# Overrun tests in single steps, the flag read before the last store, the last two blocks finished one by one

## The chip, the cores and the metric

The kernel runs on one core of a Trainium2 chip. Its time is the device time of one execution in microseconds; of several runs the median counts. The core has TensorE (PE, matmuls; PEld is its weight load), VectorE (DVE), ScalarE (ACT) and GpSimd (POOL), and SyncE (SP), which issues DMAs here. Each engine works through a queue of its own in order, and they wait for each other by semaphores.

## The reference, cut to what matters

```python
h = jnp.maximum(_layernorm(x, axis=-1), 0.0)              # 6250 nodes x 128
agg = jax.ops.segment_sum(edge_attr, dst, num_segments=6250)   # 106250 edges x 128, dst sorted
y = jnp.concatenate([agg, h], axis=1)                     # 6250 x 256
hid = jax.nn.relu(y @ W1 + b1)                            # W1: 256 x 512
out = x + (hid @ W2 + b2)                                 # W2: 512 x 128
```

All of it is float32. Every node has 17 edges on average. Since `dst` is sorted, the edges of a node lie together, but the number of edges of a node depends on the data.

## The kernel before, in words

**The sums.** The edges are cut into 276 chunks of 384 and a rest of 266. Four chunks are a round (69 rounds and the rest, which makes 70). SP loads a round of 768 KB into one of 8 slots. For each chunk VectorE compares the edges' nodes, taken relative to the first node of the chunk, with 0 to 31 (a one-hot, line 481), and TensorE multiplies the one-hots with the edges (line 767). Each chunk yields sums for 32 nodes from its first node on. ScalarE copies them out of PSUM (line 390), TensorE turns them (line 778), and VectorE adds each chunk's 32 columns into `aggT` at a column that it has loaded into a register (line 570; the registers are loaded by `load_bases`, line 554).

**The steps.** Nodes are worked in 25 blocks of 256 (the last has 106). A loop over steps k = 1 to 24 runs on every engine, written out. In step k TensorE sums the rounds for block k, VectorE adds the sums of block k-1, splits its `aggT` into two parts, builds the one-hots for block k+1, takes the statistics of x for block k+2 and adds b2 to x of block k-1 (lines 633 to 650). The first three blocks are groups of their own, and from then on two blocks make a group, so there are NS = 14 groups. In the odd steps from 5 on TensorE runs layer 1 for a group: `layer1_h` (line 802), the turns of sums and of the next x, and `layer1_agg` (line 811). ScalarE applies ReLU to four parts of `hidden` (line 406). In the even steps TensorE runs layer 2 for that group (line 823) and VectorE adds x and writes `outrow` (`finish`, line 548), which SP stores. `outrow` is single for a pair of blocks, so `finish` waits for the store of the group before it.

**The order around the change.** If the data were such that a chunk spans more than 32 nodes, or the rounds taken for a block don't hold all its edges, the sums would be incomplete. Four tests find this out, on columns of `relA`, `relB`, `relC`, `relD` (`overrun`, line 587: a maximum, a minimum and three small operations, each waiting for the one before). VectorE does A in step 6, B in 7, C and D in 8, and a comparison of the bases (line 661) in 9. In step FLAG = 11 TensorE turns the resulting columns (lines 880 to 883), VectorE takes their maximum (line 667) and writes `flag`; TensorE waits for this maximum in the next step (line 855), as the PSUM bank is shared with layer 2's output. Every engine reads the flag into a register at its end and, if it is set, runs a slow second pass, which these inputs don't need. SP reads it after the last store has landed (lines 300 to 304).

**The end.** The last group holds block 23 and block 24 (53 rows of two nodes). After its layer 1, ScalarE writes four parts of hidden, layer 2 waits for all four (line 817) and writes both blocks into PSUM bank 5, VectorE adds them one after the other (line 543) and then signals once, and SP issues two stores (lines 266 and 267):

```python
sp.wait_ge(stored, 16 * (NS - ONES + 1))        # line 300
sp.wait_ge(flag_ready, 1)                       # line 302
again = sp.value_load(flag[0:1, 0:1], min_val=0, max_val=1)
with sp.If(again > 0):
```

Of the kernel before, what the change touches and what calls it, by code (L numbers as in the profile page):

```python
# [26 lines left out]
def graph_layer(nc, x, dst, edge_attr, W1, b1, W2, b2, out):  # L27
# [62 lines left out]
        return group1(k - 1)  # L90

    EARLY = ONES
    FLAG = 11
    assert group1(FLAG) is not None and group2(FLAG) is None

    def cols_of(s):
# [7 lines left out]
    with ExitStack() as ctx:  # L104
# [64 lines left out]
        hid_ps = [bank[3], bank[4], bank[6], bank[7]]  # L169
        out_ps = bank[5]  # L170
        row_ps = bank[5]
        misc_ps = bank[7]

        dst_landed = [sem(f"dst_landed{i}") for i in range(4)]
# [44 lines left out]
        hidden_ready = sem("hidden_ready")  # L219
        out_summed = sem("out_summed")  # L220
        out_added = sem("out_added")
        over_read = sem("over_read")
        stored_one = [sem(f"stored_one{i}") for i in range(2)]
        stored = sem("stored")
# [20 lines left out]
        @block.sync  # L245
        def _(sp):
            def load(r):
                if r >= RING:
                    sp.wait_ge(round_summed, r - RING + 1)
                slot = r % RING  # L250
                if r == NR:
                    sp.dma_start(edges[0:KREST, slot, 0:GR * F], rest_v).then_inc(edges_landed[slot], 16)
                else:
                    sp.dma_start(edges[:, slot, :].rearrange("p (t n) -> p t n", t=TILES),  # L254
                                 rounds_v[:, r, :, :]).then_inc(edges_landed[slot], 16)

            def load_x(b):
                if b - 3 >= 4:
                    sp.wait_ge(x_landed[b % 4], 16 * ((b - 3) // 4))
                sp.dma_start(xs[:, b, :], x_v[:, b, :]).then_inc(x_landed[b % 4], 16)  # L260

            def store(n, s):
                sp.wait_ge(out_added, n + 1)
                bs = blocks_of(s)
                if isinstance(s, int) and s == NS - 1:
                    sp.dma_start(out_v[:, bs[0], :], outrow[:, 0, :]).then_inc(stored, 16)
                    sp.dma_start(out_last_v, outrow[0:width(NB - 1), 1, :]).then_inc(stored, 16)
                elif len(bs) == 1:
                    sp.dma_start(out_v[:, s, :], outrow[:, s % 2, :]).then_inc(stored_one[s % 2] if n < NS else stored, 16)
                else:  # L270
                    sp.dma_start(out_v[:, bass.ds(bs[0], 2), :], outrow[:, :, :]).then_inc(stored, 16)

            sp.dma_start(dstA[:, :], dst[0:P * CHUNK].rearrange("(c e) -> c e", e=CHUNK)).then_inc(dst_landed[0], 16)
            load(0)
            load(1)
            sp.dma_start(w1[:, :, :], W1.rearrange("(t p) h -> p t h", p=P)).then_inc(w1_landed, 16)
            load(2)
            sp.dma_start(xs[:, 1:3, :], x_v[:, 1:3, :]).then_inc(x_next_landed, 16)
            load(3)
            load(4)  # L280
            sp.dma_start(w2[:, :, :], W2.rearrange("(t p) f -> p t f", p=P)).then_inc(w2_landed, 16)
            for r in range(5, RING):
                load(r)
            for k in range(NB):
                if 3 <= k + 3 < NB - 1:
                    load_x(k + 3)
                if k + 3 == NB - 1:
                    sp.dma_start(xs[0:NLAST // 2, NB - 1, :], x_last_v).then_inc(x_last_landed, 16)
                early = k <= EARLY + 1
                if early and group2(k - 1) is not None:  # L290
                    store(group2(k - 1), group2(k - 1))
                for r in ROUNDS[k]:
                    if r + RING < NROUNDS:
                        load(r + RING)
                if not early and group2(k - 1) is not None:
                    store(group2(k - 1), group2(k - 1))
            store(NS - 2, NS - 2)
            store(NS - 1, NS - 1)

            sp.wait_ge(stored, 16 * (NS - ONES + 1))  # L300

            sp.wait_ge(flag_ready, 1)
            again = sp.value_load(flag[0:1, 0:1], min_val=0, max_val=1)
            with sp.If(again > 0):
                with sp.Fori(0, FULL) as c:
                    sp.wait_ge(wide_summed, c * NWIDE + 1)
                    sp.dma_start(edges[:, 0:1, 0:G * F], chunks_v[:, bass.ds(c, 1), :]).then_inc(wide_landed, 16)
                sp.wait_ge(wide_summed, FULL * NWIDE + 1)
                sp.dma_start(edges[0:KREST, 0, 0:GR * F], rest_v).then_inc(wide_landed, 16)
                for s in range(ONES):  # L310
                    store(NS + s, s)
                with sp.Fori(ONES, NS - 1) as s:
                    store(NS + s, s)
                store(2 * NS - 1, NS - 1)
                sp.wait_ge(stored, 16 * (2 * NS - ONES + 2))
# [147 lines left out]
        def _(dve):  # L463
# [64 lines left out]
            def finish(n, s):  # L528
                bs = blocks_of(s)
                dve.wait_ge(out_summed, n + 1)  # L530
                if isinstance(n, int):
                    dve.wait_ge(residual_ready, min(bs[-1] + 1, NB))
                    if len(bs) == 1 and 2 <= n < ONES:
                        dve.wait_ge(stored_one[n % 2], 16 * (n // 2))
                    if n == ONES:
                        dve.wait_ge(stored_one[0], 16 * ((ONES + 1) // 2))
                        dve.wait_ge(stored_one[1], 16 * (ONES // 2))
                    if ONES < n < NS:
                        dve.wait_ge(stored, 16 * (n - ONES))
                if isinstance(s, int) and s == NS - 1:  # L540
                    for i, b in enumerate(bs):
                        w = width(b)
                        ins = nc.vector.tensor_tensor(outrow[0:w, i, :], out_ps[0:w, i * 2 * F:(i + 1) * 2 * F],
                                                      xs[0:w, b, :], ALU.add)
                elif len(bs) == 1:
                    ins = nc.vector.tensor_tensor(outrow[:, s % 2, :], out_ps[:, 0:2 * F], xs[:, s, :], ALU.add)
                else:
                    ins = nc.vector.tensor_tensor(outrow[:, :, :], out_ps[:, :].rearrange("p (b f) -> p b f", b=2),
                                                  xs[:, bass.ds(bs[0], 2), :], ALU.add)
                ins.then_inc(out_added, 1)  # L550
# [33 lines left out]
                                      misc_ps[:, 0:G * CC].rearrange("p (g c) -> p g c", c=CC)).then_inc(done, 1)  # L584
                nc.vector.tensor_copy(relT_rest[0:KREST, :], misc_ps[0:KREST, 64:64 + GR]).then_inc(done, 1)

            def overrun(col, rel, lim):
                link(nc.vector.tensor_reduce(col[:, 1:2], rel[:, :], AX_X, ALU.max))
                link(nc.vector.tensor_reduce(col[:, 2:3], rel[:, :], AX_X, ALU.min))
                if lim is None:  # L590
                    link(nc.vector.tensor_scalar(col[:, 3:4], col[:, 0:1], float(-MEAN), float(FULL * CHUNK - SLACK),
                                                 ALU.mult, ALU.add))
                else:
                    link(nc.vector.scalar_tensor_tensor(col[:, 3:4], col[:, 0:1], float(-MEAN), lim, ALU.mult, ALU.add))
# [38 lines left out]
            for k in range(1, NB):  # L633
# [15 lines left out]
                    stats(k + 2)  # L649
                add_b2(k - 1)  # L650
                if k == 6:
                    dve.wait_ge(limit_ready, 1)
                    overrun(colA, relA, limit[:, 0:1])
                if k == 7:
                    overrun(colB, relB, limit[:, 1:2])
                if k == 8:
                    overrun(colC, relC, limit[0:CC, 2:3])
                    overrun(colD, relD, None)
                if k == 9:
                    apart = w1[0:1, 0, 0:FULL - 1]  # L660
                    link(nc.vector.tensor_tensor(apart, base_tab[:, 2:FULL + 1], base_tab[:, 0:FULL - 1],
                                                 ALU.subtract))
# [67 lines left out]
        def _(pe):  # L730
# [83 lines left out]
            def layer2(n, s):  # L814
                if not (isinstance(n, int) and n == 0):
                    pe.wait_ge(out_added, n)
                pe.wait_ge(hidden_ready, n * HT + HT)
                at = 0
                for i, b in enumerate(blocks_of(s)):
                    w = width(b)  # L820
                    for j in range(2):
                        for t in range(HT):
                            ins = nc.tensor.matmul(out_ps[0:w, (2 * i + j) * F:(2 * i + j + 1) * F],  # L823
                                                   hidden[:, t, at:at + w], w2[:, t, :], start=(t == 0), stop=(t == HT - 1))
                        at += w
                ins.then_inc(out_summed, 1)

            pe.wait_ge(ident_ready, 1)
            pe.wait_ge(rel_ready, 1)
# [116 lines left out]
```

## Time and profile before

| | us |
|---|---|
| median of 3 timed runs | 218.17 |
| lowest, highest | 218.01, 219.18 |
| the profiled execution's own time | 217.2 |
| its span | 215.2 |
| TensorE busy | 193.9 |
| VectorE busy | 132.2 |
| ScalarE busy | 84.6 |
| GpSimd busy | 43.1 |

The page gives busy times as shares of the span. The span leaves out some 2 us that the execution's own time has. TensorE's matmuls in float32 show as two records for one instruction, so a group of layer 2 with 16 products has 32 records. The granted clock of TensorE is 0.991 of full speed over the span, which is the higher of its two levels (2.4 GHz) nearly throughout.

### The profile page before, as it was taken

How to read it: one execution, taken by the hardware profiler on the slowest of the kernel's cores; microseconds unless marked ns; L12 is line 12 of the kernel's file. 1: busy time of each engine (PE TensorE's matmuls, PEld its weight loads, DVE VectorE, ACT ScalarE, POOL GpSimd, SP SyncE). 2: the span in 40 equal slices, each digit the busy share in tenths (PEclk: the TensorE clock that was granted, in tenths of full speed). 3: DMA queues.
4: the chain of work that ended last, by engine and by line, in shares of the span. 5: the costliest groups of instructions: out<-in, count | busy, mean ns of one | idle time of the engine just before them, and what ended most of it. 6: DMA issues, size and time to landing. Idle time of an engine off the chain costs nothing.

```text
span 215.2 us, 6776 instructions
## 1 busy us (share of the span) xinstructions
PE 193.9 (90%) x2549; PEld 164.8 (77%) x2549; DVE 132.2 (61%) x581; ACT 84.6 (39%) x185; POOL 43.1 (20%) x120
## 2 busy tenths in 40 slices
PE   1396999889999999699999999999999999999970
PEld 1264878778788797498798898887988988978860
DVE  1945664648767977977488577477574774741210
ACT  3031445071663532443713713734436138333400
POOL 5554020221122202102202222022022211200000
PEclk9999999999999999999999999999999999999996
DMA  6899999999999999999989999989999960100101
GB/s 222 280 389 362 375 376 374 377 379 382 388 374 387 376 381 384 376 329 309 343 266 381 345 347 377 323 296 387 293 379 373 312 225 16 49 3 0 49 5 39
DMA packets 44623, 62.55 MB, mean 291 GB/s; under 512 B 1795, under 2 KB 44294, under 8 KB 44588
## 3 DMA queue, kind: packets, MB, share of 16 engines
q1 hardware_dynamic: 44116, 61.66, 82.0%
q10 hardware_dynamic: 472, 0.43, 0.8%
q8 instruction: 22, 0.36, 0.7%
q14 instruction: 13, 0.11, 0.1%
HBM read 58.88 MB, written 3.20 MB: 288 GB/s over the span
## 4 chain that ended last, share of the span: by engine, by line
PE 64%; DMA 12%; DVE 11%; SPq 4%; issue 3%; ACT 3%; DVEq 2%; ACTq 0%
PE bank L823 17%; PE bank L767 16%; PE bank L802 13%; PE bank L811 13%; DMA edges<-in_edge_attr 7%; DMA xs<-in_x 5%; SPq L254 3%; PE bank L778 2%; DVE aggT L570 2%; DVE onehot L481 2%; PE bank L788 2%; DVEq L554 1%; ACT agg_hi L396 1%; DVE agg_lo L523 1%; ACT hidden L406 1%
## 5 line engine op out<-in xcount | busy, mean ns | idle before, releaser
L767 PE MATMUL bank<-edges,onehot 128*32 128x128 f32 x1656 | 55.1, 285 | 5.1 <-DMA edges<-in_edge_attr 4.3
L767 PEld LDWEIGHTS bank<-edges,onehot 128*32 128x32 f32 x1656 | 45.4, 114 | 12.9 <-issue 6.1
L823 PE MATMUL bank<-w,hidden 128*128 128x128 f32 (+1 forms) x400 | 48.3, 278 | 1.3 <-ACT hidden L406 0.7
L823 PEld LDWEIGHTS bank<-w,hidden 128*128 128x128 f32 (+1 forms) x400 | 45.6, 189 | 4.2 <-issue 3.2
L406 ACT ACTIVATE hidden<-bank,b_col 128x512 f32<-128x512 f32 (+2 forms) x56 | 34.2, 635 | 35.9 <-PE bank L811 35.8
L570 DVE TENSOR_TENSOR aggT<-bank,aggT 128x32 f32 x277 | 35.2, 189 | 14.3 <-issue 6.9
L375 ACT ACTIVATE xn<-xs,shift,rstd 128x128 f32<-128x128 f32 (+1 forms) x50 | 21.7, 485 | 44.1 <-POOL shift L331 44.1
L324 POOL TENSOR_SCALAR var<-meanvar 128x2 f32<-128x2 f32 (+1 forms) x25 | 7.4, 294 | 135.2 <-DVE meanvar L501 135.2
L481 DVE TENSOR_TENSOR onehot<-relT,iota 128x384 f32<-128x384 f32 x69 | 34.4, 551 | 0.0
L802 PE MATMUL bank<-hT_hi,w_hi 128*128 128x512 f32 (+2 forms) x56 | 22.4, 399 | 0.0
L517 DVE TENSOR_TENSOR hT_lo<-bank,hT_hi 128x256 fp32r<-128x256 f32 (+1 forms) x25 | 10.4, 415 | 19.3 <-ACT hT_hi L382 19.3
L811 PE MATMUL bank<-agg_hi,w_hi 128*128 128x512 f32 (+2 forms) x56 | 21.4, 382 | 0.1
L802 PE MATMUL bank<-hT_lo,w_hi 128*128 128x512 f32 (+2 forms) x56 | 20.8, 371 | 0.0
L802 PE MATMUL bank<-hT_hi,w_lo 128*128 128x512 f32 (+2 forms) x56 | 20.7, 370 | 0.0
L811 PE MATMUL bank<-agg_hi,w_lo 128*128 128x512 f32 (+2 forms) x56 | 20.4, 364 | 0.0
L811 PE MATMUL bank<-agg_lo,w_hi 128*128 128x512 f32 (+2 forms) x56 | 20.3, 363 | 0.0
L396 ACT ACTIVATE agg_hi<-aggT 128x256 fp32r<-128x256 f32 (+1 forms) x25 | 10.7, 429 | 20.3 <-DVE aggT L570 20.3
L329 POOL TENSOR_TENSOR rstd<-var,power 128x2 f32<-128x2 f32 (+1 forms) x25 | 17.7, 709 | 2.1
L523 DVE TENSOR_TENSOR agg_lo<-aggT,agg_hi 128x256 fp32r<-128x256 f32 (+1 forms) x25 | 10.5, 419 | 9.4 <-ACT agg_hi L396 9.4
L496 DVE BATCH_NORM_STATS2 halves<-xs 128x6 f32<-128x128 f32 (+1 forms) x50 | 11.9, 280 | 5.7 <-DMA xs<-in_x 5.7
L778 PE MATMUL bank<-ident,sums 128*128 128x128 f32 x70 | 12.4, 284 | 3.1 <-DVE aggT L570 1.6
L390 ACT ACTIVATE sums<-bank 128x384 f32<-128x384 f32 (+3 forms) x25 | 11.7, 466 | 6.9 <-PE bank L767 5.8
(93 smaller groups left out, 169.0 us busy)
## 6 DMA issues: line engine op xcount, KB each, us to landing
edges<-in_edge_attr SPq DMA_DIRECT2D x69, 768.0 KB, 8.9
xs<-in_x SPq DMA_DIRECT2D x21, 128.0 KB, 8.9
out_rows<-outrow SPq DMA_DIRECT2D x10, 256.0 KB
w<-in_L_gnn_W SPq DMA_DIRECT2D x1, 512.0 KB, 9.7
out_rows<-outrow SPq DMA_DIRECT2D x4, 128.0 KB, 8.4
xs<-in_x SPq DMA_DIRECT2D x1, 256.0 KB, 11.4
w<-in_L_gnn_W SPq DMA_DIRECT2D x1, 256.0 KB, 12.8
hidden<-in_dst SPq DMA_DIRECT2D x1, 192.0 KB, 3.2
```

Of the source, the lines that this page charges most:

```text
L329: nc.gpsimd.tensor_tensor(rstd[0:w, par, :], var[0:w, par, :], power[0:w, :], ALU.pow).then_inc(pow_ready, 1)
L375: ins = nc.scalar.activation(xn[0:w, par, j, :], xs[0:w, b, j * F:(j + 1) * F], ACT.Relu, bias=shift[0:w, par, j:j + 1], scale=rstd[0:w, p ...
L396: nc.scalar.activation(agg_hi[:, halves].rearrange("f (j p) -> f j p", j=2), aggT[:, bass.ds(b * BLOCK, halves.stop - halves.start)].rearr ...
L406: nc.scalar.activation(hidden[:, t, 0:cols], hid_ps[t][:, 0:cols], ACT.Relu, bias=b1_col[:, t:t + 1]).then_inc(hidden_ready, 1)
L481: nc.vector.tensor_tensor(hot, of.unsqueeze(2).to_broadcast([p, n, W]), iota[0:p, 0:W].unsqueeze(1).to_broadcast([p, n, W]), ALU.is_equal) ...
L523: nc.vector.tensor_tensor(split(agg_lo[:, halves]), aggT[:, bass.ds(b * BLOCK, halves.stop - halves.start)].rearrange("f (p j) -> f j p", ...
L570: nc.vector.tensor_tensor(win, turn_ps[:, at:at + W], win, ALU.add).then_inc(agg_added, 1)
L767: ins = nc.tensor.matmul(sums_ps[t * W:(t + 1) * W, cols], onehot[:, hots, e, :], edges[:, slot, e * F:(e + 1) * F], start=(g == 0), stop= ...
L778: ins = nc.tensor.transpose(turn_ps[:, i * F:i * F + rows], sums[0:rows, k % 2, i * F:(i + 1) * F], ident[0:rows, 0:rows])
L802: nc.tensor.matmul(hid_ps[t][:, 0:cols], wt[:, 1, to], v[:, here], start=(i == 0), stop=False)
L811: ins = nc.tensor.matmul(hid_ps[t][:, 0:cols], wt[:, 0, to], v[:, 0:cols], start=False, stop=(i == 2))
L823: ins = nc.tensor.matmul(out_ps[0:w, (2 * i + j) * F:(2 * i + j + 1) * F], hidden[:, t, at:at + w], w2[:, t, :], start=(t == 0), stop=(t = ...
```

## The change

`FLAG` goes from 11 to 19. The four tests are cut into their maximum (`overrun_top`), their minimum (`overrun_low`) and the three small operations (`overrun_limit`), which do the same as before, and stand in steps 6 to 16; the comparison of the bases goes to step 17. SP reads the flag before the last group's stores. In the last group the second block goes to PSUM bank 1 (`last_ps`, else used for the turned sums), with semaphores of its own, so that each block is added and stored by itself. In every layer 2 the first four products each wait for their own part of `hidden`.

```diff
-    FLAG = 11
+    FLAG = 19
...
+        last_ps = turn_ps
...
                     sp.dma_start(out_v[:, bs[0], :], outrow[:, 0, :]).then_inc(stored, 16)
+                    sp.wait_ge(last_added, 1 if n < NS else 2)
                     sp.dma_start(out_last_v, outrow[0:width(NB - 1), 1, :]).then_inc(stored, 16)
...
             store(NS - 2, NS - 2)
-            store(NS - 1, NS - 1)
-
-            sp.wait_ge(stored, 16 * (NS - ONES + 1))
-
             sp.wait_ge(flag_ready, 1)
             again = sp.value_load(flag[0:1, 0:1], min_val=0, max_val=1)
+            store(NS - 1, NS - 1)
+
+            sp.wait_ge(stored, 16 * (NS - ONES + 1))
             with sp.If(again > 0):
...
                 if isinstance(s, int) and s == NS - 1:
-                    for i, b in enumerate(bs):
-                        w = width(b)
-                        ins = nc.vector.tensor_tensor(outrow[0:w, i, :], out_ps[0:w, i * 2 * F:(i + 1) * 2 * F],
-                                                      xs[0:w, b, :], ALU.add)
-                elif len(bs) == 1:
+                    w = width(bs[1])
+                    nc.vector.tensor_tensor(outrow[:, 0, :], out_ps[:, 0:2 * F], xs[:, bs[0], :],
+                                            ALU.add).then_inc(out_added, 1)
+                    dve.wait_ge(last_summed, 1 if n < NS else 2)
+                    nc.vector.tensor_tensor(outrow[0:w, 1, :], last_ps[0:w, 0:2 * F], xs[0:w, bs[1], :],
+                                            ALU.add).then_inc(last_added, 1)
+                    return
+                if len(bs) == 1:
...
                 if k == 6:
+                    overrun_top(colA, relA)
+                if k == 7:
+                    overrun_low(colA, relA)
+                if k == 8:
                     dve.wait_ge(limit_ready, 1)
-                    overrun(colA, relA, limit[:, 0:1])
-                if k == 7:
-                    overrun(colB, relB, limit[:, 1:2])
-                if k == 8:
-                    overrun(colC, relC, limit[0:CC, 2:3])
-                    overrun(colD, relD, None)
+                    overrun_limit(colA, limit[:, 0:1])
                 if k == 9:
+                    overrun_top(colB, relB)
+                if k == 10:
+                    overrun_low(colB, relB)
+                if k == 11:
+                    overrun_limit(colB, limit[:, 1:2])
+                if k == 12:
+                    overrun_top(colC, relC)
+                if k == 13:
+                    overrun_low(colC, relC)
+                if k == 14:
+                    overrun_limit(colC, limit[0:CC, 2:3])
+                if k == 15:
+                    overrun_top(colD, relD)
+                    overrun_low(colD, relD)
+                if k == 16:
+                    overrun_limit(colD, None)
+                if k == 17:
                     apart = w1[0:1, 0, 0:FULL - 1]
...
             def layer2(n, s):
                 if not (isinstance(n, int) and n == 0):
                     pe.wait_ge(out_added, n)
-                pe.wait_ge(hidden_ready, n * HT + HT)
+                ends = isinstance(s, int) and s == NS - 1
                 at = 0
                 for i, b in enumerate(blocks_of(s)):
                     w = width(b)
+                    o = last_ps if ends and i else out_ps[:, 2 * i * F:2 * (i + 1) * F]
...
                     for j in range(2):
                         for t in range(HT):
-                            ins = nc.tensor.matmul(out_ps[0:w, (2 * i + j) * F:(2 * i + j + 1) * F],
-                                                   hidden[:, t, at:at + w], w2[:, t, :], start=(t == 0), stop=(t == HT - 1))
+                            if i == 0 and j == 0:
+                                pe.wait_ge(hidden_ready, n * HT + t + 1)
+                            ins = nc.tensor.matmul(o[0:w, j * F:(j + 1) * F], hidden[:, t, at:at + w], w2[:, t, :],
+                                                   start=(t == 0), stop=(t == HT - 1))
                         at += w
-                ins.then_inc(out_summed, 1)
+                    if ends and i == 0:
+                        ins.then_inc(out_summed, 1)
+                ins.then_inc(last_summed if ends else out_summed, 1)
```

## Rows read from the trace of the kernel before

**Rows 1.** The page: busy us (share) of TensorE; layer 2's weight loads, mean ns.

```profile
PE 193.9 (90%) x2549; PEld 164.8 (77%) x2549; DVE 132.2 (61%) x581; ACT 84.6 (39%) x185; POOL 43.1 (20%) x120
...
L823 PEld LDWEIGHTS bank<-w,hidden 128*128 128x128 f32 (+1 forms) x400 | 45.6, 189 | 4.2 <-issue 3.2
```

**Rows 2.** Windows: us, busy us of each engine, granted clock, DMA share, GB/s.

```profile
170.00:200.00 30.00, 30.00 (x348) 25.72 (x347) 16.46 (x78) 11.78 (x26) 4.27 (x12) 1.00 0.23 80
```

**Rows 3.** Who waited for whom, TensorE, 20 to 200 us: total, times, longest.

```profile
PE bank L778 <- DVE aggT L570: 1.6, 1, 1.6
...
PE bank L767 <- DVE over L667: 0.5, 1, 0.5
```

**Rows 4.** Windows again: the same work of TensorE in step 9 and step 11.

```profile
83.06:91.54 8.48, 6.75 (x34) 4.87 (x30) 6.96 (x31) 3.91 (x8) 1.12 (x4) 1.00 1.06 375
99.36:105.67 6.31, 6.31 (x32) 5.03 (x31) 3.60 (x14) 3.69 (x8) 1.43 (x4) 1.00 0.99 350
```

**Rows 5.** The chain of waits, steps 6 to 8: start us, us, what.

```profile
65.70 0.47 DVE colA L588
66.20 0.56 DVE colA L589
...
73.85 0.47 DVE colB L588
...
75.50 0.87 DVEq L554
...
81.66 0.46 DVE colC L588
...
84.57 0.71 DVEq L554
```

**Rows 6.** Timeline of VectorE: start us, us, operation [idle before <- releaser].

```profile
68.27 0.69 DVE L548 TENSOR_TENSOR outrow<-bank,xs 128x512 f32<-128x512 f32 x1 [0.92 <-DMA out_rows<-outrow]
...
76.58 1.69 DVE L570 TENSOR_TENSOR aggT<-bank,aggT 128x32 f32 x12 [1.08 <-issue]
...
92.61 1.69 DVE L570 TENSOR_TENSOR aggT<-bank,aggT 128x32 f32 x12 [1.10 <-issue]
...
107.82 1.69 DVE L570 TENSOR_TENSOR aggT<-bank,aggT 128x32 f32 x12 [0.93 <-issue]
```

**Rows 7.** The chain of waits, the end.

```profile
202.51 2.07 ACT hidden L406 x4
...
204.72 3.92 PE bank L823 x32
208.66 0.33 DVE outrow L543
209.00 0.41 DVE outrow L543
```

**Rows 8.** Timeline of SP, the last stores.

```profile
209.43 0.35 SPq L266 DMA_DIRECT2D out_rows<-outrow  x1
209.83 0.29 SPq L267 DMA_DIRECT2D out_rows<-outrow  x1
```

**Rows 9.** Lines 303, 304: count, ns min/median/max, first and last start us.

```profile
L303 SPq TENSOR_LOAD <-flag x1: 465/465/465, 214.0 to 214.0; - x1
...
L304 SPq COMPARE_BRANCH  x1: 45/45/45, 214.8 to 214.8; - x1
```

**Rows 10.** Windows while only the last store runs.

```profile
212.00:213.00 1.00, 0.00 (x0) 0.00 (x0) 0.00 (x0) 0.00 (x0) 0.00 (x0) 0.50 0.07 22
```

**Rows 11.** Line 757, TensorE's queue: the waits for one-hots.

```profile
L757 PEldq EVENT_SEMAPHORE  x70: 51/51/51, 6.5 to 190.3; - x70
```

**Rows 12.** The chain of waits, around the start of a layer 2.

```profile
91.61 1.45 PE bank L767 x48
93.05 3.77 PE bank L823 x32
```

**Rows 13.** Line 890: TensorE's branch on the flag.

```profile
L890 PEldq COMPARE_BRANCH  x1: 3529/3529/3529, 207.6 to 207.6; - x1
```

More of the change, by code:

```diff
@@ L221, in graph_layer @@
         out_added = sem("out_added")
+        last_summed = sem("last_summed")
+        last_added = sem("last_added")
         over_read = sem("over_read")
@@ L297, in _ @@
             store(NS - 2, NS - 2)
+            sp.wait_ge(flag_ready, 1)
+            again = sp.value_load(flag[0:1, 0:1], min_val=0, max_val=1)
             store(NS - 1, NS - 1)
             sp.wait_ge(stored, 16 * (NS - ONES + 1))
-            sp.wait_ge(flag_ready, 1)
-            again = sp.value_load(flag[0:1, 0:1], min_val=0, max_val=1)
             with sp.If(again > 0):
@@ L585, in turned_cd, with overrun_top, overrun_low, overrun_limit @@
                 nc.vector.tensor_copy(relT_rest[0:KREST, :], misc_ps[0:KREST, 64:64 + GR]).then_inc(done, 1)
-            def overrun(col, rel, lim):
+            def overrun_top(col, rel):
                 link(nc.vector.tensor_reduce(col[:, 1:2], rel[:, :], AX_X, ALU.max))
+            def overrun_low(col, rel):
                 link(nc.vector.tensor_reduce(col[:, 2:3], rel[:, :], AX_X, ALU.min))
+            def overrun_limit(col, lim):
                 if lim is None:
@@ L820, in layer2 @@
                     w = width(b)
+                    o = last_ps if ends and i else out_ps[:, 2 * i * F:2 * (i + 1) * F]
+                    if ends and i and n >= NS:
+                        pe.wait_ge(last_added, 1)
                     for j in range(2):
                         for t in range(HT):
-                            ins = nc.tensor.matmul(out_ps[0:w, (2 * i + j) * F:(2 * i + j + 1) * F],
-                                                   hidden[:, t, at:at + w], w2[:, t, :], start=(t == 0), stop=(t == HT - 1))
+                            if i == 0 and j == 0:
+                                pe.wait_ge(hidden_ready, n * HT + t + 1)
+                            ins = nc.tensor.matmul(o[0:w, j * F:(j + 1) * F], hidden[:, t, at:at + w], w2[:, t, :],
+                                                   start=(t == 0), stop=(t == HT - 1))
                         at += w
-                ins.then_inc(out_summed, 1)
+                    if ends and i == 0:
+                        ins.then_inc(out_summed, 1)
+                ins.then_inc(last_summed if ends else out_summed, 1)
             pe.wait_ge(ident_ready, 1)
```

## The prediction

> **What bounds the kernel now.** The busy table first: TensorE is busy 90% of the span [rows 1]. The windows then show a stretch from 170 to 200 us in which it is busy 30.00 of 30.00 us at a granted clock of 1.00 [rows 2]. The list of waits for TensorE between 20 and 200 us gives one large pause, 1.6 us at line 778 (the turn of a block's sums) for a VectorE add at line 570, and one of 0.5 us for the flag's reduction at line 667 [rows 3]. From the 1.6 us pause to the end TensorE has almost no gap, and the list's one row for the edges' DMA (0.4 us, once) lies at 20.6 us, before the pauses. So a microsecond that TensorE loses before about 92 us is a microsecond of the end, and so is whatever follows its last matmul. I look for the change's effect in three places: that pause, the tail after 202 us, and the cost of the new waits.
>
> **The pause in step 9.** The same work (four groups of layer 1 for x, the turns, four groups for the sums) fills 83.06 to 91.54, 8.48 us, in step 9 and 99.36 to 105.67, 6.31 us, in step 11 [rows 4]. TensorE is busy only 6.75 of the 8.48 us. The difference, 8.48 - 6.31 = 2.17 us, is the 1.6 us pause and the refilling after it. Why is VectorE late there? The chain of waits goes through it [rows 5]: in step 6 the test on colA from 65.70; in step 7 the test on colB from 73.85 to 75.50, where loading the bases starts, 1.65 us, and colA's five operations are the same; in step 8 colC and colD from 81.66 to 84.57, 2.91 us. All of it stands in front of the output add and the add of the sums that TensorE waits for.
>
> The change leaves colA's maximum, 0.47 us, in step 6, its minimum, 0.56 us, in step 7, and in step 8 the three small operations on colA, about 0.6 us with their gaps. The saving is 1.18 us in step 6, 1.09 in step 7, 2.3 in step 8. The first doesn't survive: the output add at 68.27 waited 0.92 us for the store that frees its buffer [rows 6], and would start at the same time. The others add up: VectorE is 1.1 + 2.3 = 3.4 us earlier at the end of step 8's tests. The sums of step 8 then are added by about 87.6 - 3.4 = 84.2 us, where TensorE wants them at 86.1 (its turn began at 87.76, after a pause of 1.63). Margin 1.9 us: the whole 2.17 us goes, and what is late next in step 9 is TensorE itself. Bounds: 0 if something else holds VectorE there (below), 2.2 if all goes; no reason lets it cost. I take 2.17.
>
> What the pieces cost where they land: 0.5 to 0.6 us in each step from 9 to 14, two reductions in 15 (0.35 + 0.45 us), about 0.5 in 16, about 1.1 in 17. VectorE runs two steps without tests in about 16.0 - 2.9 - 1.1 = 12.0 us (its adds of sums started at 76.58 and 92.61 [rows 6], and the tests of step 8 and 9 stood between), TensorE takes some 14.1 to 14.8 us for two. 12.0 + 1.2 stays below it, so the cover is some 1 us for each pair of steps and they cost nothing. Without that cover they would cost what they take, 7.3 us of tests in all less the 1.6 us left in steps 6 to 8: 5.7 us. Nothing in the windows points to that end.
>
> The flag's reduction moves from step 11 to 19 with its 0.5 us wait [rows 3] and its three transposes. VectorE waits in step 11 until TensorE has turned the columns and adds the sums only at 107.82 [rows 6], while TensorE asks for the next turn at 112.46: 3 us spare. Step 19 has the same rounds and blocks, so it repeats this. Cost 0; bounds -0.5 to +0.5 us.
>
> SP's queue: the loads keep their order, the only thing moved past them is the flag, and SP reaches it after its store at 200 us, when flag_ready is long set.
>
> **The tail.** ScalarE writes the four parts of hidden from 202.51 on in 2.07 us, 0.52 us each; TensorE starts layer 2 at 204.72, 0.14 us after the last [rows 7]. Its own layer 1 ends near 203.9. The 32 records from 204.72 are 16 products of two records each, 3.92 / 16 = 0.245 us for one. With waits part by part, the first is free to start once layer 1 leaves the array (about 203.9; part 0 is there at 203.1), the second follows at 204.1, the third at 204.3 (part 2 at 204.1 plus 0.14), and the fourth at 204.72 as before. Three products leave the path: 0.70 us. Less is possible if a restart costs; 0 to 0.74 (the pause), I take 0.70.
>
> Behind the last matmul the old order is: add of the first block at 208.66, 0.33 us, add of the second 0.41 us [rows 7], first store issued at 209.43, second at 209.83 [rows 8]. New: the first block's sums are complete after 8 products, near 206.1 us, its add and its store (0.35 us) run while TensorE does the second block, and bank 1 holds the second, so the two don't meet. After the last matmul stand only the second add, 0.41 us, and the second store. That removes 0.33 + 0.40 = 0.73 us. Of the first block's add the wait is new, and nothing stands behind it on VectorE but the second add; behind SP's new wait stands only the last store. Bounds 0.4 (if the first store were to run late) to 0.73; I take 0.73, since its slot is 2 us early.
>
> The flag. After the last store has landed SP loads the flag at 214.0 for 0.465 us, and branches at 214.8 [rows 9]: 0.80 us, on the path by themselves, and now done between 200.8 and 206 us. Bounds 0.4 to 0.8; I take 0.80.
>
> The last store itself: issued at 209.83, landed at 213.99, 4.16 us. While it runs the DMA engines' share is 0.07 at 22 GB/s [rows 10], that is one engine of 16. 53 KB at 22 GB/s are 2.5 us, and what is left of 3.4 us between the end of the first store's burst and 213.8 is about 0.9 us of other traffic on that engine. The shape is unchanged, so I keep 4.16, with 0.9 us to either side.
>
> In the Trainium skill (DMA: Bandwidth & Descriptors, "Why a DMA increments its semaphore by 16 and not by 1") the number of engines is the largest one up to 16 that divides the row count, so 53 rows get one; the trace agrees. [...]
>
> **The new waits.** Layer 2 runs 14 times, and 13 times its four parts are long ready, so 3 x 13 = 39 waits are added that are met. A wait of line 757 is a 51 ns instruction on TensorE's queue, 70 of them [rows 11]. Bounds: 0 and 39 x 0.051 = 2.0 us. I take 0: two rounds of sums took 1.45 us with waits between them, and layer 2 followed at 93.05, where 91.61 + 1.45 = 93.06 ends the round before, in spite of two waits between [rows 12].
>
> **Sum.** 2.17 + 0.70 + 0.73 + 0.80 = 4.40 us. The profiled execution took 217.2 us (its span is 215.2), so it would be 212.8. It lies 1 us below the median of the timed runs, 218.17; taking the sum from that gives 213.8 us.
>
> **Rivals.**
> A, the pause stays: VectorE in step 8 is held by something other than the tests. For: the output add in step 8 waits for a store too, and that of step 6 did [rows 6]. Against: that store was issued at 71 us, 11 us before. Only the tail is gained: 218.17 - 2.23 = 215.9. Chance 0.12.
> B, the last store lands late: its one engine meets other traffic, since TensorE's branch (3.529 us, [rows 13]) fetches code in the same microseconds. The price is the 0.9 us above, and the result 214.7. Chance 0.13.
> C, the branch of SP: TensorE's takes 3.529 us [rows 13] where SP's took 0.045 [rows 9]. With the flag read early, SP might pay it after its last wait: 213.8 + 3.5 = 217.3. Against: SP idles about 4 us ahead of it in both kernels. Chance 0.05. The Trainium skill (Runtime: NRT & Kernel Launch, "Instruction fetch mechanics") says that a taken branch to a page not yet held forces a fetch by DMA; TensorE's row agrees, SP's shows none.
> D, slower: each wait between the parts keeps the next weight load from going ahead, in all 13 other layer 2s. The price is one load of 0.189 us [rows 1] for each of 39 waits, 7.4 us, and the time 213.8 + 7.4 = 221.2; it decides the sign from 4.4 / 39 = 0.11 us a wait. Against: no gap at 93.05. Chance 0.04. The rule behind it: the Trainium skill (TensorE: Matmul & The Clock Gate, "Architectural detail: the array is 16× 32×32, not 1× 128×128") says that TensorE's queue can pull a weight load ahead of matmuls in flight. Whether a met wait stops that, no page says; the rounds of line 767 speak against it.
>
> **How the numbers follow.** The forecast has 0.66. About 0.5% (1.1 us) is what a measurement can tell from no change. Faster by more than that: the forecast, A and B, 0.91; within: C, 0.05; slower: D, 0.04. The range goes down to 212.7 (the store's 0.9 us, and 0.2 for the spread of the runs) and up to 216.2 (A with 0.3), leaving out C, D and B together with A.
>
> **What would show it.** Step 9 from its layer 1 to its last sum is 6.3 us, with no wait of line 778 for an add. In the tail six records of layer 2 stand before the fourth ScalarE part has ended, with a gap behind them; the last add is a single one of 0.41 us; the last store is issued some 0.02 us after it ends, where it used to be 0.42; nothing but a branch follows its landing. The length of layer 2 in mid-kernel (3.77 us [rows 12]) shows D: unchanged if I am right, over 4 us if not. I am wrong if TensorE waits for VectorE in steps 9 to 20 by more than 0.5 us in all, or if the landing takes over 5 us.

## The result, and the profile after

The changed kernel took 212.59 us (median of 4 runs, 212.05 to 212.94) beside 218.09 us for the kernel before (4 runs, 217.35 to 219.18). The ratio is 0.9742 with a 95% interval of 0.9695 to 0.9788: faster by 2.6%. The forecast was 213.8 us in a range from 212.7 to 216.2. The direction was right; the time came out 0.1 us below the range.

The profiled execution took 212.71 us with a span of 210.5 us, where the one before took 217.2 and 215.2. That is 4.5 us less, and the forecast's sum was 4.40. So most of the miss is not in the change's terms but in the number that they were taken from, as the experiments show.

The windows of the changed kernel over steps 9 and 11, the same work as in [rows 4]:

```profile
82.92:89.22 6.30, 6.30 (x33) 4.93 (x37) 4.79 (x26) 3.01 (x6) 1.42 (x4) 1.00 1.06 376
96.97:103.28 6.31, 6.31 (x34) 4.93 (x37) 4.65 (x23) 3.01 (x6) 1.39 (x4) 1.00 1.05 373
```

Step 9 now takes what step 11 takes, 6.30 us in place of 8.48. Its list of waits for TensorE between 20 and 200 us has no row in which line 804 (the turn of the sums, 778 before) waits for a VectorE add; the flag's wait is there as in [rows 3]:

```profile
PE bank L804 <- ACT sums L393: 0.7, 3, 0.2
PE bank L793 <- DVE over L693: 0.5, 1, 0.5
```

The timeline of VectorE, lines 554 (output add), 576 (adds of the sums) and the first pieces of the tests, answers to [rows 6]:

```profile
65.41 0.55 DVE L594 TENSOR_REDUCE colA<-relA 128x1 f32<-128x384 f32 x1
67.84 0.69 DVE L554 TENSOR_TENSOR outrow<-bank,xs 128x512 f32<-128x512 f32 x1 [1.89 <-DMA out_rows<-outrow]
...
73.34 0.55 DVE L597 TENSOR_REDUCE colA<-relA 128x1 f32<-128x384 f32 x1
...
82.13 0.69 DVE L554 TENSOR_TENSOR outrow<-bank,xs 128x512 f32<-128x512 f32 x1 [1.26 <-DMA out_rows<-outrow]
82.74 1.58 DVE L576 TENSOR_TENSOR aggT<-bank,aggT 128x32 f32 x12
```

In step 6 the time saved goes into the wait for the store, 1.89 us where it was 0.92. In step 8 the output add waits for a store as well, 1.26 us, for a store issued at 70.97 us. Yet the sums are added by 84.3 us, 1.6 us before TensorE asks for them at 85.92.

The end of the chain of waits, then SP's timeline, then SP's and TensorE's branches (lines 307 and 923), for [rows 7 to 9] and [rows 13]:

```profile
199.62 1.99 PE bank L837 x12
201.62 3.93 PE bank L854 x32
...
205.57 0.42 DVE outrow L548
```

```profile
204.14 0.35 SPq L269 DMA_DIRECT2D out_rows<-outrow  x1
206.02 0.28 SPq L271 DMA_DIRECT2D out_rows<-outrow  x1
```

```profile
L307 SPq COMPARE_BRANCH  x1: 45/45/45, 210.1 to 210.1; - x1
...
L923 PEldq COMPARE_BRANCH  x1: 3689/3689/3689, 204.5 to 204.5; - x1
```

Layer 2 follows layer 1 with no gap, one add of 0.42 us stands behind it, the last store is issued as it ends, and the branch follows the landing at 210.1. From the last matmul's end to the last store it was 1.2 us, now 0.47.

### The profile page after: what moved, and what is told of

The parts are those of the page before. It is cut to its first block, busy times and chain, and to the rows that moved or that the text cites. A ratio compares the mean times of both kernels' runs of the same rounds, so it can differ in the third digit from the quotient of the medians.

```text
span 210.5 us, 6775 instructions
## 1 busy us (share of the span) xinstructions
PE 193.7 (92%) x2549; PEld 164.9 (78%) x2549; DVE 131.5 (62%) x581; ACT 84.7 (40%) x185; POOL 43.0 (20%) x120
## 4 chain that ended last, share of the span: by engine, by line
PE 79%; DMA 11%; SPq 3%; DVE 2%; ACT 1%; issue 1%; DVEq 0%; ACTq 0%
PE bank L854 21%; PE bank L793 20%; PE bank L828 16%; PE bank L837 15%; DMA edges<-in_edge_attr 6%; DMA xs<-in_x 5%; PE bank L804 3%; SPq L257 3%; PE bank L814 2%; PE bank L786 1%; ACT xn L378 1%; DVE aggT L576 1%; SPq L282 0%; ACT sums L393 0%; SPq L280 0%
## 5 line engine op out<-in xcount | busy, mean ns | idle before, releaser
L828 PEld LDWEIGHTS bank<-hT_hi,w_hi 128*128 128x128 f32 x56 | 10.9, 194 | 4.2 <-issue 2.8
```

The lines of the kernel that those rows point to most:

```text
L828: nc.tensor.matmul(hid_ps[t][:, 0:cols], wt[:, 1, to], v[:, here], start=(i == 0), stop=False)
```

## The experiments

Times are medians with the range of the runs. Each group of kernels ran on one chip, with runs of the kernel before beside it; ratios are against those. The first group (e0, e1, e6, e2) had 20 runs of the kernel before, median 217.17 us. The second (a0, e3, e4, e8) had 11 with 218.0, the third (x1, x2, x3, d1) 11 with 217.17, the fourth (v1, e8 again) 17 with 218.45.

**e0, the kernel before against itself.** No edit.

> The kernel before once more, against itself. Theory 1 (the terms of the profile, 4.7 us in all, are the gain, and the 5.5 us between the medians carry 0.8 us of scatter of the kernel before): its median comes out nearer to the profiled 217.2 us than to 218.1, and the pause at the turn of the sums in step 9 is 1.6 us again. Theory 2 (the pause differs from execution to execution, and the profiled one had a short one): a pause clearly other than 1.6 us, and spans of the timed runs that scatter by over 1 us.

Measured: 217.31 us (216.64 to 219.13, 12 runs), ratio 1.0018 (0.9986 to 1.005), pause 1.7 us in the profile. Both theories got something: the median is 0.8 us below that of the first comparison, and the runs spread over 2.5 us in two heaps. Of all 71 timed runs of the kernel before in these experiments, 45 took 216.3 to 218.1 us (median 216.93), and 26 took 218.3 to 219.6 (median 218.78). In time alone the gap between the heaps is only 0.2 us wide; the clock parts them better. The upper 26 all have a mean granted clock of 0.982 to 0.989, of the lower 45 all but two have more than 0.989.

**e1, the tests back in steps 6 to 9.**

```diff
 # on the changed kernel
-                if k == 6:
-                    overrun_top(colA, relA)
-                if k == 7:
-                    overrun_low(colA, relA)
...
+                if k == 6:
+                    dve.wait_ge(limit_ready, 1)
+                    overrun(colA, relA, limit[:, 0:1])
+                if k == 7:
+                    overrun(colB, relB, limit[:, 1:2])
+                if k == 8:
+                    overrun(colC, relC, limit[0:CC, 2:3])
+                    overrun(colD, relD, None)
+                if k == 9:
```

> The changed kernel with the tests of A to D back in steps 6 to 8 and the bases' comparison in 9 (the flag's step stays 19). Theory 1: the pause of step 9 is back and the time rises by 2.2 us over the changed kernel, to about 214.8 us, some 2.5 to 3 us below the kernel before. Theory 2: by over 3 us. Rival 3 (the pause had another cause than the tests): no change, 212.6.

Measured: 215.28 us (214.74 to 218.02, 9 runs), ratio 0.9914 (0.9877 to 0.9952). The runs are again in two heaps, five from 214.7 to 215.3 us and three from 216.5 to 217.4, and two of these three have a clock of 0.987 or less. The ninth, 218.02 us at 0.979, is left out of the ratio. The lower heap is 2.2 us above the changed kernel (212.69, median of its 10 runs in both groups), the upper 4 us. Rival 3 is out.

The ninth run is the profiled one, and its trace shows what the pause can do. First TensorE's longest wait, then windows (the granted clock is the third column from the right), then the chain of waits:

```profile
PE bank L784 <- DVE aggT L576: 1.9, 1, 1.9
```

```profile
88.00:91.00 3.00, 2.38 (x10) 1.84 (x11) 2.71 (x13) 1.02 (x2) 0.00 (x0) 0.85 1.06 373
91.00:95.00 4.00, 4.00 (x48) 3.08 (x50) 2.70 (x16) 2.48 (x6) 1.47 (x4) 0.69 0.69 248
95.00:100.00 5.00, 5.00 (x68) 4.63 (x64) 3.75 (x12) 1.32 (x5) 0.82 (x3) 1.00 0.80 247
```

```profile
89.36 4.61 PE bank L817 x12
```

TensorE waits 1.9 us for the sums and starts again at 88.5. The clock then stands at 0.50 (1.2 GHz) from about 90.1 to 93.5 us, and the twelve products of layer 1 take 4.61 us where they take 2.75 in the changed kernel: 1.86 us more. That is the distance between the heaps of before, 218.78 - 216.93 = 1.85 us. As an estimate, 3.4 us at half the clock lower the mean over 215 us by 0.008, beside median clocks of 0.994 and 0.988 in the two heaps.

**e6, only the tests spread, on the kernel before.**

```diff
 # on the kernel before
-    FLAG = 11
+    FLAG = 19
 # and the tests as in the change, steps 6 to 17
```

> The kernel before with only the tests spread over steps 6 to 17 and the flag in step 19. Theory 1: 2.2 to 2.4 us less than before, some 215.8 us beside 218.1. Theory 2: over 3 us less. Rival 3: nothing.

Measured: 214.94 us (214.45 to 215.35, 6 runs), ratio 0.9879 (0.9849 to 0.991), which is 2.6 us with an interval of 2.0 to 3.3. By the medians of the group it is 2.2 us, against the lower heap of before 2.0. This edit moves the flag's step as well; e1, which leaves it at 19, gives 2.2 us for the tests alone. One heap is left, 0.9 us wide. No run of any kernel here without the pause had a mean clock under 0.990, in 64 runs of nine kernels.

**d1, a longer pause.**

```diff
 # on the kernel before
                 if k == 8:
+                    for _ in range(8):
+                        link(nc.vector.tensor_reduce(colC[:, 1:2], relC[:, :], AX_X, ALU.max))
                     overrun(colC, relC, limit[0:CC, 2:3])
```

> The kernel before with eight more reductions in step 8, 0.56 us each, so that the pause of TensorE in step 9 is 1.6 + 4.5 = 6.1 us. Theory 2 (a pause also costs clock behind it): the granted clock falls to its lower level after the pause, the products behind it take up to twice as long, and the time rises by 4.5 us and 1.5 to 2 us more, to 223 us or more. Theory 1 (a pause costs its length alone): 217.0 + 4.5 = 221.5 us.

Measured: 223.28 us (222.16 to 223.92, 6 runs), ratio 1.0271 (1.0233 to 1.0309), every run at a clock of 0.975 to 0.981. Windows of its profile; the granted clock is the third column from the right:

```profile
86.00:89.00 3.00, 0.03 (x1) 0.00 (x0) 2.72 (x10) 0.00 (x0) 0.00 (x0) 1.00 1.06 378
89.00:92.00 3.00, 0.00 (x0) 0.00 (x0) 1.98 (x13) 0.00 (x0) 0.00 (x0) 0.64 1.05 371
92.00:94.00 2.00, 1.63 (x7) 1.56 (x8) 1.82 (x6) 0.44 (x1) 0.00 (x0) 0.50 0.79 286
94.00:96.00 2.00, 2.00 (x6) 1.54 (x5) 1.83 (x9) 0.69 (x1) 0.91 (x3) 0.50 0.11 38
96.00:98.00 2.00, 2.00 (x15) 1.38 (x17) 0.90 (x7) 1.47 (x3) 0.56 (x2) 0.84 0.01 2
```

and its chain of waits there:

```profile
92.37 0.87 PE bank L780 x3
93.24 0.43 PE bank L790 x2
93.67 4.20 PE bank L813 x12
```

TensorE is idle from 86 to 92.4 us, the clock falls to 0.50 (1.2 GHz) within the pause and stays there until after 96. The three turns take 0.87 us where they take 0.33, the twelve products 4.20 where they take 2.75. That is 0.5 + 0.2 + 1.45 = 2.2 us behind the pause. Against the lower heap of before the time rose by 6.35 us, for 4.5 us of reductions and a pause 4.7 us longer: some 1.7 to 1.9 us is the clock's. Theory 2 holds. The Trainium skill (TensorE: Matmul & The Clock Gate, "What's actually happening") says that a monitor of the array's activity halves its clock after idleness; the trace agrees, 0.50 within a pause of 6.3 us.

That the upper heap of the kernel before is this fall behind its own pause has good support. e1's trace shows the fall behind the same pause, at the price of 1.86 us; the heap has that size and the lower clock, and it goes with the pause. What is not shown is the fall in the kernel before itself: its four profiles (the first, e0, b1 and b2) have pauses of 1.6, 1.7, 1.8 and 1.5 us, and are all of the lower heap at a clock of 1.00 in step 9. What decides between a fall and none is open.

A rival for the heap is a fall near the start. e1's trace has one at 22 to 25 us too, behind waits of 0.7 and 1.0 us. The trace of e8 run again (below) has one at 24.5 to 28, behind a wait of 2.3 us, and v1's has one at 24 to 28, behind a wait of 2.5. These need no pause in step 9. But in the 64 runs without that pause they are rare enough that none has a clock under 0.990, where 28 of the 71 runs of the kernel before have one, so they don't make the heap.

**b1 and b2, two more profiles of the kernel before.** No edit.

> A look at one execution of the kernel before. If it is one above 218.3 us (three in ten were), theory 2 expects a granted clock under 1.00 in the 6 us behind the pause of step 9 and 1.5 to 2 us more for the products there; theory 1 expects the time elsewhere. If it is below, it tells nothing new.

> One more execution of the kernel before, for the same: above 218.3 us, theory 2 expects the clock to fall behind the pause of step 9, and theory 1 the time elsewhere; below, it tells nothing new.

Measured: 217.09 and 216.57 us, both of the lower heap, with pauses of 1.8 and 1.5 us and no fall of the clock behind them.

**e2, the flag read late again.**

```diff
 # on the changed kernel
-            sp.wait_ge(flag_ready, 1)
-            again = sp.value_load(flag[0:1, 0:1], min_val=0, max_val=1)
             store(NS - 1, NS - 1)

             sp.wait_ge(stored, 16 * (NS - ONES + 1))
+            sp.wait_ge(flag_ready, 1)
+            again = sp.value_load(flag[0:1, 0:1], min_val=0, max_val=1)
```

> The changed kernel with SP's load of the flag after the last store's landing again. Theory 1: 0.75 to 0.8 us more than the changed kernel, about 213.4 us. A rival: under 0.3 us, if the load can hide behind something else at the end.

Measured: 212.82 us (212.78 to 213.6, 6 runs), ratio 0.9796 (0.9765 to 0.9827), span 210.9. The lowest span is 0.9 us above the changed kernel's 210.0, the time only 0.1 above its 212.69. A surprise: what the span leaves out is 1.8 to 1.9 us here and 1.9 to 2.8 us in the changed kernel.

**e3, one wait for all four parts.**

```diff
 # on the changed kernel
+                pe.wait_ge(hidden_ready, n * HT + HT)
                 ends = isinstance(s, int) and s == NS - 1
...
-                            if i == 0 and j == 0:
-                                pe.wait_ge(hidden_ready, n * HT + t + 1)
```

> The changed kernel with layer 2 waiting for all four parts of hidden at once, as before. The prediction's term: 0.70 us more than the changed kernel (its trace shows 0.73), 12.9 to 13.0 beside 212.2. Rival: the wait by parts costs in the other 13 layer 2s and this kernel gets back part of it, so less than 0.5 us.

(The figures "12.9 to 13.0" there stand for 212.9 to 213.0.) Measured: 213.20 us (212.78 to 213.45), ratio 0.9775 (0.9724 to 0.9827). That is 0.5 us above the changed kernel's 212.69, but level with the 213.17 that it had in the same group (a0, below), so the time alone doesn't show the term. The median span does, 211.05 beside 210.5. Its chain of waits ends

```profile
199.97 2.07 ACT hidden L409 x4
202.04 0.14 issue
202.18 3.92 PE bank L853 x32
```

The gap before layer 2 is back, and in mid-kernel a layer 2 takes 3.77 us in both: the 39 waits that are met cost nothing.

**e4, the last two blocks together.**

```diff
 # on the changed kernel: PSUM, adds, signal and stores of the last group as in the kernel before
-                    o = last_ps if ends and i else out_ps[:, 2 * i * F:2 * (i + 1) * F]
+                    o = out_ps[:, 2 * i * F:2 * (i + 1) * F]
```

> The changed kernel with the last two blocks in one PSUM bank, added one after the other, signalled once and then stored. The prediction's term: 0.73 us more than the changed kernel, and the last store is issued 1.17 us after the last matmul's end where the changed kernel has 0.47. Rival: the last store's landing is what counts, and it gets shorter when it follows another store at once, so less than 0.4 us.

Measured: 213.29 us (212.65 to 213.82), ratio 0.9778 (0.9725 to 0.983): 0.6 us above 212.69 and 0.1 above 213.17, with a median span of 211.25 us. In its profile the last store goes out 1.19 us after the last matmul, against 0.47:

```profile
206.64 0.35 SPq L269 DMA_DIRECT2D out_rows<-outrow  x1
207.04 0.33 SPq L270 DMA_DIRECT2D out_rows<-outrow  x1
```

**e8, the last store cut into 48 and 5 rows.**

```diff
 # on the changed kernel (the new semaphore is waited for with the other)
-                    sp.dma_start(out_last_v, outrow[0:width(NB - 1), 1, :]).then_inc(stored, 16)
+                    w = width(NB - 1)
+                    cut = w - w % 16
+                    sp.dma_start(out_last_v[0:cut, :], outrow[0:cut, 1, :]).then_inc(stored, 16)
+                    sp.dma_start(out_last_v[cut:w, :], outrow[cut:w, 1, :]).then_inc(stored_tail, 16)
```

> The changed kernel with the last store of 53 rows cut into one of 48 and one of 5 rows, to see what the landing costs: its 53 packets run one after the other on one DMA engine, 3.0 of 4.1 us. If the engine's row is what holds the end, the two land 1.8 to 2.3 us sooner, 210.0 to 210.4 us beside 212.2, and the branch follows the last issue by some 2 us. Rival (the landing is a fixed latency, or other traffic): under 0.5 us gained, or 0.35 us lost for the second issue.

Measured: 212.83 us (212.55 to 213.81, 6 runs), ratio 0.9774 (0.9721 to 0.9827); the changed kernel had 213.17 in the same group (a0, below). SP's timeline, its wait for the stores, its branch and TensorE's:

```profile
205.73 0.33 SPq L274 DMA_DIRECT2D out_rows<-outrow  x1
206.10 0.36 SPq L275 DMA_DIRECT2D out_rows<-outrow  x1
```

```profile
SPq L311 <- DMA out_rows<-outrow: 0.9, 1, 0.9
```

```profile
L312 SPq COMPARE_BRANCH  x1: 45/45/45, 207.5 to 207.5; - x1
...
L929 PEldq COMPARE_BRANCH  x1: 3429/3429/3429, 204.2 to 204.2; - x1
```

The landing came 2.6 us sooner (0.3 of it because the stores began sooner in this profile), 1.0 us after the last issue, and the span fell to 208.0 us; in the other five runs it was 209.1 to 209.6, beside 210.5 for the changed kernel. The time did not move: 3.4 to 4.6 us now lie outside the span. Something else ends last, and it doesn't show in the span.

**a0, the changed kernel again.**

> The changed kernel again, for more runs beside the same runs of the kernel before. Theory 1 (the terms read in the two traces, 4.7 us): about 217.2 - 4.7 = 212.5 us, or with the tests alone at 2.6 us as measured, 212.1. Theory 2 (in some executions of the kernel before the granted clock falls behind the pause of step 9, which the changed kernel doesn't have): besides that, its runs lie within 1 us of each other, where those of before spread over 2.8 us, and none has a clock under 0.99.

Measured: 213.17 us (212.54 to 214.19, 6 runs) beside 218.0, ratio 0.9785 (0.973 to 0.9841). No clock under 0.993. Its spread is 1.65 us, more than expected; part of it is what the span leaves out (1.9 to 2.8 us), and the spans themselves go from 210.0 to 211.8. Only one of these runs has a trace, so where the others spent it is not shown.

**x1, x2 and x3, the second pass left out.** x1 is e8 without the second pass, its flag loads and branches on every engine; x2 is e8 without it on TensorE alone; x3 is the changed kernel without it on every engine.

```diff
-            again = pe.value_load(flag[0:1, 0:1], min_val=0, max_val=1)
-            with pe.If(again > 0):
...
```

> The kernel with the last store cut into 48 and 5 rows, and the second pass with its flag loads and branches left out on all engines. That kernel's span fell by 2.5 us and its time by nothing: what the span leaves out grew from 2.1 to 3.4 us and more. Theory F (a second path ends last: TensorE's branch over the second pass takes 3.5 us and fetches code, and the execution ends some 8.3 us after the branch begins): without it the time is the span and 2.0 us, 209.5 to 210.3. Rival G (the end outside the span is as it is, whatever the branches do, as long as the last matmul stands where it stands): 212.6 again.

> The same with the second pass left out on TensorE alone. Theory F names TensorE: as with all engines, 209.5 to 210.3 us. Rival H (another engine's branch or code fetch is as late as TensorE's): over 211.5 us.

> The changed kernel, last store whole, with the second pass left out on all engines. Theory F: the store's landing near 210.05 us then is the only path, and the time is that and 2.0 + 0.4 us, 212.2 to 212.4, a little under the changed kernel and with less scatter (what the span leaves out is 2.0 us in every run, where it was 1.9 to 2.8). Rival G: as the changed kernel, 212.5 to 214.2.

Measured: x1 209.77 us (209.4 to 211.52), ratio 0.967 (0.963 to 0.9709); x2 210.92 us (209.46 to 211.89), 0.9721 (0.9686 to 0.9755); x3 212.26 us (212.03 to 213.2), 0.9775 (0.9741 to 0.9809). What the span leaves out is 1.75 to 1.9 us in all 18 runs. Theory F holds in its core: without the branch over the second pass the short store is worth 2.5 us (212.26 - 209.77), and with TensorE's alone gone the time is already 1.9 us under e8's and nothing is left outside the span but 1.8 us. x2's median lies between the two theories, 0.6 us above what F forecast and 0.6 below what H did. Since its time outside the span is 1.8 us, the 0.6 us lies inside the span: 207.7 us in its profile and 208.9 to 210.1 in the other five runs, as in e8, where x1 has 207.6 to 208.1 in five of its six. Which engine holds that is open.

**v1, TensorE's branch ahead of the last group,** and e8 again beside it.

```diff
 # on e8
+            pe.wait_ge(flag_ready, 1)
+            again = pe.value_load(flag[0:1, 0:1], min_val=0, max_val=1)
+            with pe.If(again > 0):
+                last_group()        # layer1_h, layer1_agg, layer2 of the last group
                 ...                 # and the second pass
+            with pe.If(again < 1):
+                last_group()
```

> The kernel with the last store cut into 48 and 5 rows, and TensorE's flag load and branch moved ahead of the last group: if the flag is set, it runs the last group and the second pass, else the last group alone. Theory F: the branch's 3.5 us now stand about 2 us ahead of the work TensorE has in its queue, so TensorE pauses for some 1.5 us before the last group, but nothing of it is left behind the last matmul: about 209.8 + 1.5 = 211.3 us, 1.3 us below the kernel with the cut store, with 1.8 to 2.1 us outside the span. If the pause costs clock, 212 to 213. Rival G: 212.6 + 1.5 = 214.

> The kernel with the last store cut into 48 and 5 rows again, beside the former: 212.6 to 213.0 us, with 3.4 to 4.6 us outside the span.

Measured: v1 219.26 us (218.04 to 219.72), ratio 1.0045 (1.0012 to 1.0078); e8 213.06 us (212.36 to 214.46), 0.9786 (0.9732 to 0.984), with 3.2 to 4.7 us outside the span. The branch, the wait it left and the chain of v1:

```profile
L930 PEldq COMPARE_BRANCH  x1: 3366/3366/3366, 196.8 to 196.8; - x1
```

```profile
PE bank L834 <- issue: 5.1, 1, 5.1
```

```profile
198.11 5.12 issue
203.23 3.99 PE bank L834 x12
```

F's 1.5 us were wrong by far. The branch ends at 200.2, but the next product starts at 203.23: behind the taken branch TensorE stands for 3 us more, with no wait for another engine in the list. The pause of 5.1 us also costs clock, since the twelve products take 3.99 us where they took 2.18 (0.66 granted between 200 and 210 us). Nothing is left behind the end, 1.8 to 1.9 us outside the span. This accounts for the other kernels, if TensorE stands as long behind the branch there: it is ready only some 3.4 + 3 us after its branch begins. In the changed kernel that is 204.5 + 6.7 = 211.2 us, later than SP's 210.1, and it lies outside the span. The traces allow a test of this. A profile's branch start and length, 3.03 us and the 1.85 us that x1 to x3 leave outside add up to estimates of 212.5 us for e8, 214.0 for e8 again, 213.1 for the changed kernel, 212.8 for a0, 212.7 for e2, 213.8 for e3 and 213.5 for e4; these runs took 212.55, 214.16, 212.71, 212.67, 212.78, 213.37 and 213.46, within 0.45 us in all seven. The Trainium skill (Runtime: NRT & Kernel Launch, "Instruction fetch mechanics") has a taken branch wait for a fetch; v1's rows agree: in each of its two waits of about 3 us lies one 16 KB packet of the instruction queue.

## Why the prediction was right and where it failed

**The pause in step 9, 2.17 us.** Right: 8.48 to 6.30 us in the trace, 2.2 us between e1's lower heap and the changed kernel, 2.0 between before's lower heap and e6. Its cause too. The bounds, "0 if something else holds VectorE there (below), 2.2 if all goes", failed on the far side: in some executions the pause had a second price, about 1.9 us of clock, seen in e1's trace (1.86 us), made regular by d1 (1.7 to 1.9) and fitted by the upper heap (1.85 us, in 26 of 71 runs). The sum didn't have this term.

**From which time the sum is taken.** This is the step that put the time outside the range: "it lies 1 us below the median of the timed runs, 218.17; taking the sum from that gives 213.8". The profile was of the lower heap, and the forecast from its 217.2, which the prediction also gives, was 212.8; the profiled run took 212.71 and the median is 212.59. The median of the three runs lay at the gap between the heaps, and the changed kernel has no upper heap, so taking the sum from that median put 1 us on top that the changed kernel's runs don't have. Runs at 218.01, 218.17 and 219.18 against a profile at 217.2 were the sign. From heap to heap the gain is 216.93 - 212.69 = 4.24 us, against 4.40 forecast.

**The tests where they land, the flag's step, the 39 waits: 0.** Right: no new wait of TensorE, the flag's wait is 0.5 us in step 19, and a layer 2 in mid-kernel takes 3.77 us with the waits and without (e3). Rival D is out.

**The tail.** In the trace each term is as forecast: 0.73 for three products (0.70), 0.73 for adds and stores, some 0.8 for the flag, and a landing of 4.05 us in place of 4.16. In the time they are worth less: undone one by one they cost 0.5 (e3), 0.6 (e4) and 0.1 us (e2) against 212.69, and 0.0 and 0.1 for e3 and e4 against the 213.17 of their own group, so none is clear of the spread of the runs. The spans show 0.5 to 0.75 us for each. All of the tail together is 214.94 - 212.69 = 2.25 us (e6 against the changed kernel); with 212.59 or 213.17 for the changed kernel it is 2.35 or 1.8, so that this meets the forecast's 2.23 to 0.02 is luck. There is no more to be had on that path, since what follows TensorE's branch ends as late. C had named the wrong engine: SP's branch stayed at 0.045 us, TensorE's was the limit, and the forecast saw its 3.529 us row without counting what follows it. A's mechanism was there. The forecast held against it that the store was issued at 71 us, 11 us before; it was issued at 70.97 and held the add until 82.13 all the same, with 1.6 us to spare. B didn't happen.

So the 5.5 us of the first comparison are some 2.0 from the pause, 2.25 from the tail, and the rest, by what is left, from where its four runs of before fell: one in the upper heap, two at the gap, one in the lower. Their clocks were not recorded, so this last part is argued.

## What to carry to other kernels

A pause of TensorE of under 2 us can cost nearly twice its length, and doesn't in most executions, so look at each timed run's clock, and ask whether the times of the kernel before fall in two heaps, before a sum is taken from their median. A span isn't the execution: where the time outside it grows as the span falls, a path outside the trace has become the end. Work on the last microseconds pays only up to the next path, here a branch over code that never runs, and moving such a branch into the kernel cost 6 us.

## What the runs showed of the hardware

- A store of 53 rows ran on one DMA engine of 16 (a share of 0.07 at 22 GB/s before) and landed 4.05 us after its issue began; cut into 48 and 5 rows the last of the two landed 1.3 us after its issue began (e8).
- A taken branch on TensorE over the second pass took 3.3 to 3.9 us in the traces that have it, and the next product came 3 us after that (v1).
- The granted clock was at 0.50 by the end of a pause of 6.3 us and came back some 4 us after work had begun again (d1).
- Behind a pause of 1.9 us it fell to 0.50 some 1.6 us after work had begun again and stayed there for 3.4 us (e1); behind pauses of 1.5 to 1.8 us in four profiles of the kernel before it did not fall.
